# adaLN block on one core: normalised rows of batches 2 and 3 turned by VectorE blocks and a DMA between quadrants in place of TensorE transposes

## What is computed

```python
h = _layernorm(x) * (1 + ca) + sa
x = x + ga * attention(h, Wqkv, bqkv, Wo, bo)      # one head of width 128, softmax over 512 keys
h = _layernorm(x) * (1 + cb) + sb
x = x + gb * (h @ W_up.T + top-1 expert's rank-8 delta)
```

## Time and profile before

| | us |
|---|---|
| median of three runs | 194.16 |
| profiled execution, its own time | 194.07 |
| profiled execution, span of the trace | 192.2 |
| TensorE busy in the span | 177.0 (92%) |
| VectorE busy | 137.6 (72%) |
| ScalarE busy | 90.9 (47%) |
| GpSimd busy | 79.5 (41%) |
| DMA engines, mean busy share of 16 | 29% |

### The profile page before, as it was taken

The page is one execution under the profiler, slowest core; times in us unless marked ns, Lnnn a source line. Parts: engine busy times, 40 slices in busy tenths (PEclk is TensorE's granted clock), DMA queues, the critical chain, the costliest instruction groups (busy, mean ns, idle before and its releaser), DMA issues.

```text
span 192.2 us, 2846 instructions
## 1 busy us (share of the span) xinstructions
PE 177.0 (92%) x951; PEld 139.0 (72%) x951; DVE 137.6 (72%) x339; ACT 90.9 (47%) x172; POOL 79.5 (41%) x106
## 2 busy tenths in 40 slices
PE   6897999989998789986999999999999999988991
PEld 6874757866766658864888788878887887767770
DVE  1839748799989854796885478569566493986964
ACT  3355045954168976420746596113565622456110
POOL 3544200278154980005778940015696000332750
PEclk9999999999999999999999999999999999999999
DMA  5999996910033000022021500000232000001315
GB/s 173 381 385 386 382 269 108 398 64 5 0 79 141 3 2 0 0 76 95 0 109 55 164 3 0 0 0 3 109 122 42 3 0 3 0 0 55 144 42 196
DMA packets 12221, 19.21 MB, mean 100 GB/s; under 512 B 2812, under 2 KB 3328, under 8 KB 12208
## 3 DMA queue, kind: packets, MB, share of 16 engines
q1 hardware_dynamic: 12208, 19.05, 29.2%
HBM read 14.83 MB, written 4.21 MB: 99 GB/s over the span
## 4 chain that ended last, share of the span: by engine, by line
PE 45%; DVE 4%; issue 1%; ACT 1%; POOL 1%; DVEq 0%; POOLq 0%
PE bank L349 31%; PE bank L476 2%; PE bank L503 2%; PE bank L579 1%; DVE xs L1152 1%; DVE stats L1159 1%; PE bank L527 1%; PE bank L529 1%; PE bank L461 1%; PE bank L455 1%; PE bank L458 1%; PE bank L432 1%; PE bank L557 1%; DVE f_gb L1217 1%; ACT h2hi L844 1%
## 5 line engine op out<-in xcount | busy, mean ns | idle before, releaser
L1402 POOL TENSOR_TENSOR rstd<-var_eps,neg_half 128x1 f32<-128x1 f32 x16 | 8.8, 553 | 47.3 <-DVE var_eps L1163 47.3
L349 PE MATMUL bank<-wup_lo,h2hi 128*128 128x512 f32 x64 | 26.7, 417 | 0.6 <-DVE lbw L1085 0.6
L825 ACT ACTIVATE xn_p<-xs,shift,rstd 128x512 f32<-128x512 f32 x16 | 12.9, 815 | 27.7 <-POOL shift L1405 27.7
L349 PE MATMUL bank<-wup_hi,h2hi 128*128 128x512 f32 x64 | 25.3, 395 | 0.0
L349 PE MATMUL bank<-wup_hi,h2lo 128*128 128x512 f32 x64 | 25.2, 393 | 0.0
L1417 POOL TENSOR_TENSOR xs<-xs,f_gb 128x512 f32<-128x512 f32 x14 | 17.9, 1292 | 7.2 <-DVE f_gb L1217 7.2
L349 PE MATMUL bank<-h1lo,wqkv_hi 128*128 128x512 f32 x48 | 19.7, 411 | 1.2 <-ACT wqkv_hi L818 1.2
L1394 POOL TENSOR_TENSOR xs<-xs,gabo 128x512 f32<-128x512 f32 x16 | 20.3, 1302 | 0.1
L349 PE MATMUL bank<-h1hi,wqkv_hi 128*128 128x512 f32 x48 | 19.0, 395 | 0.0
L349 PE MATMUL bank<-h1hi,wqkv_lo 128*128 128x512 f32 x48 | 18.9, 394 | 0.0
L1379 POOL TENSOR_TENSOR wo_ga<-wo_raw,ga_bc 128x512 f32<-128x512 f32 x4 | 5.1, 1280 | 32.2 <-DMA ga_bc<-gates_dram 17.3
(11 more groups left out here) (180 smaller groups left out, 421.7 us busy)
## 6 DMA issues: line engine op xcount, KB each, us to landing
out_dram<-xs SPq DMA_DIRECT2D x16, 256.0 KB, 2.0
stage<-in_L_wmod_dram SPq DMA_DIRECT2D x3, 1024.0 KB, 6.8
xs<-in_L_wmod_dram SPq DMA_DIRECT2D x3, 1024.0 KB, 9.0
xs<-in_L_attn_x_dram SPq DMA_DIRECT2D x3, 1024.0 KB, 6.7
xs<-in_L_attn_x_dram SPq DMA_DIRECT2D x2, 512.0 KB, 3.9
f_gb<-in_L_ffn_W_up_dram SPq DMA_DIRECT2D x1, 1024.0 KB, 10.5
gb_bc<-gates_dram SPq DMA_DIRECT2D x4, 256.0 KB, 3.6
xn_p<-in_L_attn_Wqkv_dram SPq DMA_DIRECT2D x4, 192.0 KB, 7.9
```

The source lines that it names most:

```text
L349: mm = nc.tensor.matmul(dst, w, m, start=first and i == 0, stop=last and i == total - 1)
L825: nc.scalar.activation(xn2_p[:, t, :], xs[:, b, t, :], ACT.Identity, bias=shift[:, 1, t:t + 1], scale=rstd[:, 1, t:t + 1]).then_inc(S["xn2 ...
L1402: nc.gpsimd.tensor_tensor(rstd[:, 1, t:t + 1], var_eps[:, 1, t:t + 1], neg_half[:, 0:1], ALU.pow).then_inc(S["ln2_rstd"], 1)
```

## The change

For batches 2 and 3 TensorE's 16 x1 transposes each are left out. In their place:

- ScalarE writes the normalised rows of token tile t into `xn1` in an order of 32-column blocks (`xn1_blocks`).
- VectorE turns every 32x32 block of the tile in its own 32 partitions (`turn_blocks`, one instruction for a tile, four for a batch).
- SP moves blocks between the four groups of 32 partitions: 16 DMAs of 32 rows of 2 KB each (`move_turned`), all behind one wait for the four VectorE instructions, into `stage`, which is free by then.
- ScalarE scales the turned tensor in place by 1 + ca (`x1_scale`, four instructions) and rounds it to `h1hi` (`h1_high`, four). VectorE subtracts to get `h1lo`, now with both inputs in SBUF.

Also moved: `ln1_normalise(2)` stands behind the softmax of batch 1 and not ahead of it; the statistics of batch 3 stand ahead of `pt_low(1)`; `gate_columns("gb")` behind it and `gate_rows_evacuate("gb")` behind `choose_expert(0)`; `h1_low` stands behind `o_low` (for batch 3 half of it ahead of `o_low`); a quarter of `up(b-1, 1)` stands ahead of P's transposes; the banks of fb and gzb are swapped, and `fb_hi` lies in `c_rows`.

```diff
@@ -25,6 +25,11 @@
 BY_ACT = 3
+TURNED = 2
+BLOCK = 32
+NB = P // BLOCK
 QUARTER = 32
 SCORE_SCALE = float(D) ** -0.5
 GATE_FLOOR = 0.25
...
@@ -55,7 +60,7 @@
         (7, "Y", 0, 0), (4, "Y", 0, 1), (6, "Y", 0, 2), (5, "Y", 0, 3), (2, "mod", 3),
         (7, "gateA"), (4, "loraB"), (2, "modT", 3),
         (7, "x2T", 0, 0), (4, "x2T", 0, 1), (6, "x2T", 0, 2), (5, "x2T", 0, 3),
-        (2, "fb"), (7, "gzb"), (4, "gz", 0),
+        (7, "fb"), (2, "gzb"), (4, "gz", 0),
     ]
     m, f = (0, 1, 3, 6, 5), (2, 7, 4)
     for b in range(1, B):
...
@@ -64,8 +69,6 @@
         if b == 1:
             order += [(f[2], "gate_row", "gb")]
         order += [(f[0], "F", b - 1, 0)]
-        if not last:
-            order += [(m[kt], "x1T", b + 1, kt) for kt in range(NK)]
         order += [(m[4], "zl", b - 1)] + [(m[t], "PT", b, t) for t in range(NT)] + [(f[1], "F", b - 1, 1)]
         order += [(m[0], "O", b), (m[4], "zT", b - 1), (f[2], "F", b - 1, 2)]
         order += [(m[i], "Y", b, t) for t, i in enumerate((1, 2, 3, 0))] + [(f[0], "F", b - 1, 3)]
...
@@ -162,7 +166,12 @@
         f_gb = sb("f_gb", [P, 4, H])
         lora_b_rep = xn1[:, 0, 0:NK * ZROWS].rearrange("p (k a z) -> p k a z", k=NK, a=3)
-        fb_hi = stage[:, 0, :]
+        fb_hi = c_rows
+        xn1_blocks = xn1[:].rearrange("p t h -> p (t h)").rearrange("p (a k t i) -> p a k t i", a=NB, k=NK, t=NT)
+        turned_in = {b: (stage if b > 1 else h2lo)[:].bitcast(F32).rearrange("p t h -> p (t h)").rearrange(
+            "p (c k t i) -> p c k t i", c=NB, k=NK, t=NT) for b in range(TURNED, B)}
         mod_rows = gb_bc
         stats = sb("stats", [P, 2, NT, 6])
         moments = sb("moments", [P, 2, NT, 2])
...
@@ -236,6 +246,20 @@
             return range(2 * half[0], 2 * half[0] + 2) if half else range(NT)
+        def turned_columns(b, kt):
+            return turned_in[b][:, :, kt].rearrange("p c t i -> p t c i")
+        def by_blocks(columns):
+            return columns.rearrange("p (t c i) -> p t c i", t=NT, c=NB)
+        def xn1_free(engine, b):
+            if b <= TURNED:
+                engine.wait_ge(S["x1T_psum"], NK * b)
+            else:
+                engine.wait_ge(turned_moved, 16 * NB * NB * (b - TURNED))
         def xn1_done(engine, b, t=NT):
             if b == 0:
...
@@ -280,7 +304,17 @@
                 to, ready = ((ga_bc, ga_bc_in), (gb_bc, gb_bc_in))[i]
                 sp.dma_start(to[:, b % 2, :], gates_dram[i, b].partition_broadcast(P)).then_inc(ready[b % 2], 16)
-            sp.dma_start(c_row[:], c).then_inc(c_in, 16)
+            def move_turned(b):
+                sp.wait_ge(S["xn1_turned"], NT * (b - TURNED + 1))
+                if b > max(TURNED, 2):
+                    sp.wait_ge(S["h1_lo"], NK * b)
+                for a in range(NB):
+                    for c in range(NB):
+                        sp.dma_start(turned_in[b][a * BLOCK:(a + 1) * BLOCK, c],
+                                     xn1_blocks[c * BLOCK:(c + 1) * BLOCK, a]).then_inc(turned_moved, 16)
+            sp.dma_start(c_rows[0:B, :], c).then_inc(c_in, 16)
             for i in range(2):
                 sp.dma_start(xs[:, 0, 2 * i:2 * i + 2], x_v[0, :, 2 * i:2 * i + 2, :]).then_inc(x0_in[i], 16)
             load_section("ca")
...
@@ -312,12 +346,15 @@
             spread_gate(0, 1)
             wait_used(3)
             sp.dma_start(xs[:, 3], x_v[3]).then_inc(x_in[3], 16)
+            move_turned(2)
             write_gate(1)
             spread_gate(1, 0)
             spread_gate(1, 1)
             for b in range(B):
                 if b + 2 < B:
                     spread_gate(0, b + 2)
+                if b == 1:
+                    move_turned(3)
                 for t in range(NT):
                     if b == LAST and t >= 2:
                         sp.wait_ge(last_out_ready, t - 1)
...
@@ -677,15 +714,11 @@
                 if b > 1:
                     scores(b)
                     v_transposes(b)
-                if last:
-                    up(b - 1, 0)
-                else:
-                    up(b - 1, 0, (0, 1))
-                    x1_transposes(b + 1)
-                    up(b - 1, 0, (2, 3))
+                up(b - 1, 0)
                 z_to_tokens(b - 1)
+                up(b - 1, 1, (0,))
                 p_transposes(b)
-                up(b - 1, 1)
+                up(b - 1, 1, (1, 2, 3))
                 if b == 1:
                     gate_to_rows("gb")
                 pv(b)
...
@@ -736,13 +769,24 @@
         def _(act):
             def h1_high(b, kts=range(NK)):
                 for kt in kts:
+                    if b and kt == 0:
+                        act.wait_ge(S["qkv_psum"], 3 * b)
+                    if b >= TURNED:
+                        act.wait_ge(S["x1_scaled"], NK * (b - TURNED) + kt + 1)
+                        nc.scalar.activation(by_blocks(h1hi[:, kt, :]), turned_columns(b, kt),
+                                             ACT.Copy).then_inc(S["h1_hi"], 1)
+                        continue
                     act.wait_ge(S["x1T_psum"], NK * b + kt + 1)
                     if b == 0 and kt % 2 == 0:
                         act.wait_ge(S["modT_ready"], 1 + kt // 2)
-                    if b and kt == 0:
-                        act.wait_ge(S["qkv_psum"], 3 * b)
                     nc.scalar.activation(h1hi[:, kt, :], at("x1T", b, kt)[:], ACT.Copy,
                                          scale=modT["ca"][:, kt, b:b + 1]).then_inc(S["h1_hi"], 1)
+            def x1_scale(b):
+                act.wait_ge(turned_moved, 16 * NB * NB * (b - TURNED + 1))
+                for kt in range(NK):
+                    nc.scalar.activation(turned_in[b][:, :, kt], turned_in[b][:, :, kt], ACT.Copy,
+                                         scale=modT["ca"][:, kt, b:b + 1]).then_inc(S["x1_scaled"], 1)
             def modulation_rows(g):
                 act.wait_ge(S["mod_psum"], g + 1)
...
@@ -807,10 +851,11 @@
                 for t in range(NT):
                     act.wait_ge(S["ln1_shift"], BY_ACT + NT * (b - 2) + t + 1)
                     if t == 0:
-                        act.wait_ge(S["x1T_psum"], NK * b)
+                        xn1_free(act, b)
                         if b == 2:
                             act.wait_ge(S["loraB_psum"], 1)
-                    nc.scalar.activation(xn1[:, t, :], xs[:, b, t, :], ACT.Identity, bias=shift[:, 0, t:t + 1],
+                    nc.scalar.activation(xn1_blocks[:, :, :, t].rearrange("p a k i -> p k a i"),
+                                         xs[:, b, t, :].rearrange("p (k a i) -> p k a i", k=NK, a=NB), ACT.Identity, bias=shift[:, 0, t:t + 1],
                                          scale=rstd[:, 0, t:t + 1]).then_inc(S["xn1_by_act"], 1)
             def wqkv_high(kt):
...
@@ -913,23 +958,27 @@
             h2_high(0)
             qkv_evacuate(1)
             wo_high(1)
-            ln1_normalise(2)
             for b in range(1, B):
                 last = b == LAST
                 softmax(b, (0, 1, 2))
                 v_evacuate(b)
                 softmax(b, (3,))
                 if b == 1:
+                    ln1_normalise(2)
+                    gz_evacuate(0)
                     act.wait_ge(S["fb_psum"], 1)
                     nc.scalar.activation(fb_hi[ZROWS:P, :].bitcast(F32R), at("fb")[ZROWS:P, :], ACT.Copy).then_inc(S["fb_hi_ready"], 1)
-                    gz_evacuate(0)
+                if b == 2:
+                    x1_scale(3)
+                pt_high(b)
+                if b == 1:
+                    x1_scale(2)
                 if not last:
                     h1_high(b + 1)
-                pt_high(b)
                 o_high(b)
                 zT_evacuate(b - 1)
-                if b + 2 < B:
-                    ln1_normalise(b + 2)
+                if b == 1:
+                    ln1_normalise(3)
                 if not last:
                     ln2_normalise(b)
                     wo_high(b + 1)
...
@@ -1088,6 +1137,10 @@
             def h1_low(b, kts=range(NK)):
                 for kt in kts:
                     dve.wait_ge(S["h1_hi"], NK * b + kt + 1)
+                    if b >= TURNED:
+                        nc.vector.tensor_tensor(by_blocks(h1lo[:, kt, :]), turned_columns(b, kt),
+                                                by_blocks(h1hi[:, kt, :].bitcast(F32)), ALU.subtract).then_inc(S["h1_lo"], 1)
+                        continue
                     nc.vector.scalar_tensor_tensor(h1lo[:, kt, :], at("x1T", b, kt)[:], modT["ca"][:, kt, b:b + 1],
                                                    h1hi[:, kt, :].bitcast(F32), ALU.mult,
                                                    ALU.subtract).then_inc(S["h1_lo"], 1)
...
@@ -1119,6 +1172,11 @@
                 nc.vector.tensor_tensor(v_lo[:].rearrange("p t d -> p (t d)"), at("V", b)[:],
                                         v_hi[:].bitcast(F32).rearrange("p t d -> p (t d)"),
```

(29 more changed lines are left out.)

2 lines of the change are left out of this document (1 added, 1 removed).

## The result

The changed kernel took **207.71 us**, median of four runs (207.09 to 208.68), the kernel before 194.08 in the same comparison: ratio 1.071, interval 1.0658 to 1.0762. The forecast had 196.4 and a range up to 199.5. The profiled execution took 208.26 us, span 206.5. All 11.9 us between that execution and the forecast arise in rounds 1 and 2.

What follows compares the result with a forecast made beforehand. TensorE was taken as the bound, busy throughout round 2. Round 1 -0.5, round 2's transposes -1.75, wait before pv(2) +4.3, longer VectorE chain +0.3: +2.3 us, from 194.07 to 196.4 us, range 193.5 to 199.5.

Steps and rivals of the forecast that it cites:

- the price of the DMAs: SP's 16 DMAs between quadrants per batch: 15 issue steps of 0.37 us plus 2.0 us landing, 7.6 us.
- D: Time from VectorE's last block transpose to the last DMA landing: 7.6 us, ends 5.9 and 10.4, break-even about 5.2.
- Round 1: Output projection at about 87.0 instead of 89.02, little of it surviving; the round gives 0.5 us.
- scalings: x1_scale on ScalarE, four 128x512 reads of SBUF per batch: 2.6 us, ending at 83.2 in round 1.
- Round 2: TensorE stands 4.3 us before pv(2), which starts at 123.6; x2_transposes(2) comes 2.3 us later than before.
- rival 3: TensorE's clock falls to 1.2 GHz in the 4.3 us wait of round 2: 200.5 or 198.5 us; chance 0.10.
- the end of round 1: GpSimd's start moves from 88.53 to 89.1, it runs without pause, and x2_transposes(1) starts at 100.7.
- Rival 1: Batch 3's turn is through before TensorE asks: 192.1 us at 3.4 us or less, 193.3 at 4.5; chance 0.17.
- Rival 4: SP's queue is slower than taken, 9 us and over from last transpose to last landing: 198 to 199.6 us; chance 0.07.
- block transposes: VectorE's turn of a 128x512 tile: 0.65 us each, 2.6 us for the four of a batch.
- the gates: VectorE writes the rows of gb only behind choose_expert(0) in round 1, 0.6 us later.
- the removal of 1.75 us a round: TensorE's 16 x1 transposes taken out twice, 1.75 us each: at most 3.5 us gained.

Runs made afterwards that it cites:

- e6: Changed kernel with the same bytes moved in four DMAs of 128 rows, quadrants not exchanged, so rows wrongly placed: 196.84 us, ratio 1.0158.
- e7: Changed kernel with the same 16 DMAs reading x from DRAM instead of SBUF, so those batches are not normalised: 201.76 us, ratio 1.0414.
- e1: Changed kernel with ScalarE's four scalings of batch 3 behind phi(2) instead of ahead of it: 203.41 us, ratio 1.050.
- e5: Changed kernel with 34 small identity matmuls in a free bank ahead of pv(2), filling TensorE's wait: 205.80 us, ratio 1.063.
- e8: Changed kernel with half of each batch's 16 DMAs issued from GpSimd's queue behind its additions: 200.45 us, ratio 1.0247.

## Why the prediction was wrong

- **The step that failed is the price of the DMAs**, "15 x 0.37 + 2.0 = 7.6 us". The landing was right (2.05). The spacing was 0.63 us, above even the high end of 0.45: D was 11.6 and 12.4 us, 4.0 and 4.8 too much. I took the cheapest issues of the earlier trace rows, none of which reads SBUF in a burst, for a burst of 16, and let the count of rows decide, which e6 shows doesn't matter. The trace of before had loads in bursts at its start, at 0.46 to 0.52 us an issue (lines at e7), which I left out; they would have given 15 x 0.52 + 2.0 = 9.8 us.
- **Round 1**, forecast -0.5, was +3.8. The burst put the scalings at 85.0 instead of 80.6 (0.4 of it from late transposes), the projection at 91.14 instead of 87.0 and x2T(1) at 105.11 instead of 100.7. h1_low(2), taken at 2.6 us, took 3.88 beside GpSimd, 1.3 us on the chain, which GpSimd's wait partly absorbed.
- **Round 2**, forecast +2.8 over its start, was +10.3. The mechanism was as put: phi behind the scalings behind the DMAs, plo 3.1 us behind phi's start, pv released by plo. It came at 132.62 instead of 123.6, 9.0 us late, of which 4.4 us is round 1 and 4.8 the longer D, less 0.2 in between. e1 confirms it: phi ahead of the scalings takes 6.1 us out.
- **The clock** was rival 3, a chance of 0.10, priced for a wait of 4.3 us. With 8.7 us of waiting it came, and cost 2.8 us, between the 2.05 and 4.1 worked out. In e6 it came behind 4.4 us too, so the 4.3 us forecast might well have brought it; that was not run. The Trainium skill ("TensorE: Matmul & The Clock Gate", HAM oscillation) had warned of it; the trace agrees with 12 matmuls in 5.46 us, and e5 takes it away.
- 9.0 us at pv(2) + 2.8 us (clock) = 11.8 us, by which x2T(2) missed its forecast.
- **A second step was off, hidden under the first: the end of round 1.** GpSimd's start was forecast for 89.1, with no loss of clock behind TensorE's wait for the last xn_p. Where D doesn't hide it, it was 89.52 (e8) and 90.82 (e6), x2T(1) came at 101.04 and 102.26 and not 100.7, and the low clock took 1.4 and 1.9 us of the transposes behind it. So even a D of 7.6 us would likely not have given 196.4 us: e6, with D 3.2 us shorter, took 196.84 us (196.20 in the profiled execution). Rival 1, with 193.3 us for a D of 4.5, failed on D, and by e6 a short D alone wouldn't have brought it.
- Rival 4, "the queue is slower", was the right direction and ended at 199.6, which is a D of 10.8 us by its own slope, and left the clock to rival 3. Both had one cause: the same D makes the wait that lowers the clock. I should have joined them.
- **Right:** block transposes at 0.62 (0.65), scalings at 2.56 (2.6), the gates 1.0 us later (0.6), the removal of 1.75 us a round worth nothing where another engine is late.
- **A slip in its numbers:** "+1 to +3.5 us by the bounds of D" doesn't fit its own ends, 194.7 and 199.2 us, which are +0.6 and +5.1 us. The result lies outside both.

## What to carry to other kernels

Price a burst of small DMAs by issues in a burst, one price for each whatever its rows, and put nothing urgent behind an engine instruction that waits for the last of them. A wait on TensorE that lowers its clock costs the wait and slow matmuls behind it; count both as one case. Before work is moved off a full engine, look for what its waits are made of. Here three moves (a load ahead of others in the queue, two banks swapped, statistics in idle time) and one wait that kept GpSimd off a small VectorE instruction made the kernel 1.2% faster; the change with the turn made it 7% slower.
